# Perceiver block on one core: weight pieces split during the context, part of the output projection moved into attention

## The reference

```python
x = x + xattn(ctx, layernorm(x))   # latents attend to 8192 context tokens and to themselves
x = x + attn_layers(layernorm(x))  # 8 layers of linear attention and a 2048-wide MLP
x = x + ffn(layernorm(x))          # 16 groups of experts

def xattn(ctx, lat):               # 8 heads of 64
    q = ln(lat) @ Wq
    k, v = split(concat(ln(ctx), ln(lat)) @ Wkv)   # context keys are rotated
    return (softmax(q k^T / 8) v) @ Wo

def layer(x):
    Q, K, v = elu(x Wq + bq) + 1, elu(x Wk + bk) + 1, x Wv + bv
    V = Q * sum(K * v) / (Q * sum(K) + eps)
    x = norm(gelu(V Wo + bo) + x)
    return norm(gelu(gelu(x Wf1 + bf1) Wf2 + bf2) + x)
```

## Time and profile before

| | |
|---|---|
| median of 3 runs | 2258.04 us (2256.72 to 2260.37) |
| the profiled execution | 2262.21 us |
| its span in the profile | 2260.3 us |
| mean granted TensorE clock | 0.987 |
| TensorE matmul busy | 2143.5 us, 95% |
| VectorE busy | 1650.3 us, 73% |
| ScalarE busy | 1100.0 us, 49% |
| GpSimd busy | 992.3 us, 44% |

### The profile page before, as it was taken

How to read it: one execution, slowest core, us unless ns; L and a number is a source line. 1 busy time by engine, 2 the same in 40 slices (tenths; PEclk the granted TensorE clock), 3 DMA queues, 4 the chain that set the end, 5 groups by cost and what they waited for, 6 DMA issues and landing times. The chain is left out here.

```text
span 2260.3 us, 37940 instructions
## 1 busy us (share of the span) xinstructions
PE 2143.5 (95%) x12744; PEld 1083.5 (48%) x12843; DVE 1650.3 (73%) x2384; ACT 1100.0 (49%) x1722; POOL 992.3 (44%) x682
## 2 busy tenths in 40 slices
PE   5899999989999999999799999999999999999977
PEld 2344444433333333323365575757566575756633
DVE  7687777659989999999575756667575666757663
ACT  4122322234445544555364755646475565646545
POOL 0234434459999999978320402222040222204044
PEclk9999999999999999999899999999999999999989
DMA  3344454333333432432223333342323334233313
GB/s 115 131 150 140 152 178 143 130 120 87 114 116 91 121 102 84 121 96 81 102 87 113 94 131 104 101 142 86 113 84 131 104 118 134 76 112 97 122 38 113
DMA packets 159853, 252.74 MB, mean 112 GB/s; under 512 B 11506, under 2 KB 63986, under 8 KB 159730
## 3 DMA queue, kind: packets, MB, share of 16 engines
q1 hardware_dynamic: 159730, 250.96, 34.8%
HBM read 211.73 MB, written 36.70 MB: 110 GB/s over the span
## 5 line engine op out<-in xcount | busy, mean ns | idle before, releaser
L1345 POOL TENSOR_TENSOR l_rstd<-l_var_eps,neg_half 128x1 f32<-128x1 f32 x71 | 67.3, 948 | 835.0 <-DVE l_var_eps L1399 835.0
L66 PE MATMUL l_mm<-xt_hi,wt_hi 128*128 128x256 f16 (+3 forms) x1568 | 413.2, 275 | 6.7 <-DVE xt_lo L1388 5.6
L68 PE MATMUL l_mm<-xt_hi,wt_lo 128*128 128x256 f16 (+3 forms) x1568 | 413.1, 275 | 0.4
L67 PE MATMUL l_mm<-xt_lo,wt_hi 128*128 128x256 bf16 (+3 forms) x1560 | 410.5, 275 | 0.0
L878 DVE TENSOR_REDUCE pmax<-mx 128x1024 f32 (+1 forms) x196 | 239.3, 1221 | 29.4 <-PE mx L1069 20.0
L68 PE MATMUL l_tok<-wt_hi,h_lo 128*128 128x512 f16 x576 | 218.8, 380 | 1.7
L1627 ACT ACTIVATE wt_hi<-stage 128x512 f16<-128x512 f32 x384 | 213.6, 615 | 5.2 <-DMA stage<-in_L_attn_Wf 5.1
L1082 PE MATMUL sc<-q_hi,res 128*128 128x512 f16 x544 | 208.4, 383 | 6.4 <-ACT f_hi L992 3.2
L1083 PE MATMUL sc<-q_lo,res 65*128 65x512 f16 x544 | 207.5, 381 | 0.0
L66 PE MATMUL l_tok<-wt_hi,h_hi 128*128 128x512 f16 x512 | 194.6, 380 | 0.0
L67 PE MATMUL l_tok<-wt_lo,h_hi 128*128 128x512 bf16 x480 | 182.4, 380 | 0.0
(11 more groups left out here) (321 smaller groups left out, 4874.3 us busy)
## 6 DMA issues: line engine op xcount, KB each, us to landing
stage<-in_L_attn_Wf SPq DMA_DIRECT2D x64, 1024.0 KB, 5.2
keys<-wt_hi SPq DMA_DIRECT2D x136, 128.0 KB
res<-keys SPq DMA_DIRECT2D x68, 256.0 KB, 3.4
vb<-values SPq DMA_DIRECT2D x68, 256.0 KB, 5.6
stage<-in_ctx SPq DMA_DIRECT2D x16, 1024.0 KB, 9.8
values<-wt_lo SPq DMA_DIRECT2D x16, 1024.0 KB
stage<-in_L_ffn_f SPq DMA_DIRECT2D x16, 1024.0 KB, 5.3
res<-keys SPq DMA_DIRECT2D x68, 128.0 KB, 5.4
```

The source lines that it names most:

```text
L66: pe.matmul(out, lh, rh, start=first, stop=False, **kw)
L67: pe.matmul(out, lh, rl, start=False, stop=False, **kw)
L68: return pe.matmul(out, ll, rh, start=False, stop=last, **kw)
L1345: g.tensor_tensor(rstd[:, t:t + 1], var_eps[:, t:t + 1], k.neg_half[:, 0:1], ALU.pow).then_inc(rstd_done, 1)
```

## The change

1. **Six weight chunks are made in the context phase.** In context blocks 3, 5, 7, 9, 11 and 13 ScalarE makes the four high pieces of a chunk after its last value copy, and GpSimd the four low pieces as its last work of the block. SP loads each chunk (1 MB) into `k.res` one block earlier, after the store of the values. They are `wv`, `wo` and `wf1`, which go to slots 6 to 11. As `k.res` also holds the key buffers of attention, their constant row is written by VectorE in context block 15 instead of the first phase, and SP's first key loads wait for the last low piece. SP's loop is written out.
2. **Attention makes only three chunks, in pair 3.** Pairs 1 and 2 have no loads, high or low pieces. In pair 3 the last two low pieces stand behind the last sums.
3. **Nine twelfths of the output projection stand at attention's end.** The two score banks become shared with the layers' `mm`. TensorE projects pairs 0 and 1 of tile 0 ahead of the last row sums, and the rest of pairs 0 to 2 of all tiles behind them. The layers do pair 3 alone.
4. **Order at the layers' start.** The bias transposes go to the banks `tok`, TensorE's wait for the bias instructions goes away, and VectorE splits tiles 0 to 2 ahead of the sum of tile 3.

```diff
@@ context_phase, SP @@
+                    if u == 0 and 1 <= i <= EARLY_CHUNKS:
+                        if i > 1:
+                            sp.wait_ge(w_lo, 4 * (i - 1))
+                        sp.dma_start(k.res[:], k.first_weights(STAGES - 1 + i).rearrange("(c p) n -> p c n", p=P)).then_inc(w_in, 16)
-                over_blocks(sp, body)
+                for b in range(CTX_BLOCKS):
+                    body(b // 2, b % 2)
@@ context_phase, GpSimd, end of body @@
+                    if has_pieces(i, u):
+                        for n in range(4):
+                            pool.wait_ge(w_hi, 4 * i + n - 3)
+                            g.tensor_tensor(lo_pieces[:, piece_at(i, n), :], k.res[:, n:n + 1, :],
+                                            hi_pieces[:, piece_at(i, n), :], ALU.subtract).then_inc(w_lo, 1)
@@ context_phase, VectorE @@
+                    if isinstance(i, int) and (i, u) == (HALF_BLOCKS - 1, 1):
+                        dve.wait_ge(w_lo, 4 * EARLY_CHUNKS)
+                        for n in range(2):
+                            v.memset(k.kh[n][HD:HD + 1], M_UNIT).then_inc(units, 1)
@@ context_phase, ScalarE, end of body @@
                     values(i, u, 3)
+                    if has_pieces(i, u):
+                        act.wait_ge(w_in, 16 * i)
+                        for n in range(4):
+                            a.activation(hi_pieces[:, piece_at(i, n), :], k.res[:, n:n + 1, :], ACT.Copy).then_inc(w_hi, 1)
@@ attention_phase, VectorE @@
-                            block_work(p, b, b > FIRST_PIECE)
+                            block_work(p, b, FIRST_PIECE < b < KB - 1)
...
-                        weight_low(p, KB)
+                        for b in range(KB - 1, KB + 1):
+                            weight_low(p, b)
                         continue
-                    with dve.Fori(0, FIRST_PIECE + 1 if p else TURN) as b:
+                    with dve.Fori(0, TURN) as b:
                         block_work(p, b, False)
-                    if p:
-                        dve.wait_ge(w_staged, 16 * STAGES * p)
-                        with dve.Fori(FIRST_PIECE + 1, TURN) as b:
-                            block_work(p, b, True)
                     pair_max(p + 1)
                     for b in range(TURN, KB):
-                        block_work(p, b, p > 0)
-                    if p:
-                        weight_low(p, KB)
+                        block_work(p, b, False)
@@ attention_phase, TensorE @@
+                def project(t, c):
+                    toks = slice(t * P, (t + 1) * P)
+                    product3(t_, sc[t // 2][:, t % 2 * TOK:(t % 2 + 1) * TOK], (k.o_hi[:, c, toks], k.o_lo[:, c, toks]),
+                             (k.wt_hi[:, XWO, c, :], k.wt_lo[:, XWO, c, :]), c == 0, False)
...
+                for c in range(2):
+                    project(0, c)
                 row_sums(PAIRS - 1)
+                for t in range(TT):
+                    for c in range(0 if t else 2, PAIRS - 1):
+                        project(t, c)
@@ layers_phase, VectorE @@
                 stream_norm(1)
+                low(0, 0)
+                stream_norm(2)
+                low(1, 1)
+                low(2, 2)
                 stream_stats(3)
-                stream_norm(2)
...
                 stream_norm(3)
-                for t in range(TT - 1):
-                    low(t, t)
                 dve.sem_inc(w_lo_dve, 32)
@@ layers_phase, TensorE @@
-                    for c in range(PAIRS):
-                        x = product3(t_, mm[t][:], (k.o_hi[:, c, rows], k.o_lo[:, c, rows]),
-                                     (wt_hi[:, XWO, c, :], wt_lo[:, XWO, c, :]), c == 0, c == PAIRS - 1)
-                    x.then_inc(projected, 1)
+                    c = PAIRS - 1
+                    product3(t_, mm[t][:], (k.o_hi[:, c, rows], k.o_lo[:, c, rows]),
+                             (wt_hi[:, XWO, c, :], wt_lo[:, XWO, c, :]), False, True).then_inc(projected, 1)
...
-                pe.wait_ge(cols_done, 4)
```

More of the change, by code:

```diff
@@ L35 @@
 MAX_COLS = KB + 2
+EARLY_CHUNKS = 6
 PIECES = 4 * STAGES
@@ L181, in norm @@
                                         ALU.subtract, ALU.mult).then_inc(norm_done, 1)
-                for n in range(2):
-                    v.memset(k.kh[n][HD:HD + 1], M_UNIT).then_inc(consts, 1)
                 norm(0, k.x_sb, z, EPS_OUTER)
@@ L265, in _ @@
                 t_ = nc.tensor
-                pe.wait_ge(consts, 6)
+                pe.wait_ge(consts, 4)
                 pe.wait_ge(norm_done, 2 * TT)
@@ L357, in context_phase @@
         passed = sem("c_passed")
+        units, w_in, w_hi, w_lo = (nc.alloc_semaphore(n) for n in ("c_units", "c_w_in", "c_w_hi", "c_w_lo"))
+        k.spare_semaphores += [units, w_in, w_hi, w_lo]
+        hi_pieces, lo_pieces = (w[:].rearrange("p a c n -> p (a c) n") for w in (k.wt_hi, k.wt_lo))
         ctx_v = k.ctx.rearrange("(b t p) d -> b p t d", p=P, t=SUB)
@@ L384, in earlier_units, with has_pieces, piece_at @@
             return TT * b + (2 * TT if not isinstance(b, int) or b >= 3 else TT if b == 2 else 0)
+        def has_pieces(i, u):
+            return u == 1 and (not isinstance(i, int) or 1 <= i <= EARLY_CHUNKS)
+        def piece_at(i, n):
+            return bass.ds(4 * (XWO + STAGES - 1 + i) + n, 1)
         def late_pair(i, u):
@@ L442, in body @@
                     if not before_end(i, u, 1):
+                        sp.wait_ge(w_lo, 4 * EARLY_CHUNKS)
                         for n in range(2):
@@ L749, in attention_phase @@
         o_inv, o_t = rows(k.h_lo, 12, 2), rows(k.h_lo, 14, 2)
-        sc = [pb(f"sc{n}", [P, 2 * TOK], F32) for n in range(2)]
+        sc = k.scores
         mx = pb("mx", [P, 2, BLK], F32)
@@ L794, in load_weights @@
                 def load_weights(p, n):
-                    if not 1 <= p < PAIRS:
-                        return
-                    if p > 1:
-                        sp.wait_ge(w_lo, PIECES * (p - 2) + CH * (n + 1))
-                    c = STAGES * (p - 1) + n
-                    w = ((k.xwo, k.wk[0], k.wq_l[0], k.wv[0], k.wo[0])[c] if c < 5
-                         else k.wf1[0, :, (c - 5) * D:(c - 4) * D])
-                    sp.dma_start(k.stage[:, n], w.rearrange("(c p) n -> p c n", p=P)).then_inc(w_staged, 16)
+                    if p == PAIRS - 1:
+                        sp.dma_start(k.stage[:, n], k.first_weights(n).rearrange("(c p) n -> p c n", p=P)).then_inc(w_staged, 16)
                 def two_on(p, b):
@@ L1031, in _ @@
                         continue
-                    with act.Fori(2, FIRST_PIECE if p else TURN) as b:
+                    with act.Fori(2, TURN) as b:
                         for j in range(SUB):
                             exponential(p, b, j)
-                    if p:
-                        act.wait_ge(w_staged, 16 * STAGES * p)
-                        with act.Fori(FIRST_PIECE, TURN) as b:
-                            for j in range(SUB):
-                                exponential(p, b, j)
-                            weight_high(p, b)
                     for b in range(TURN, KB):
@@ L1228, in layers_phase @@
         kv_neg = sb("kv_neg", [P, CH], F32)
-        mm = [pb(f"l_mm{n}", [P, D], F32) for n in range(4)]
+        mm = [k.scores[n // 2][:, n % 2 * D:(n % 2 + 1) * D] for n in range(4)]
         tok = [pb(f"l_tok{n}", [P, D], F32) for n in range(2)]
@@ L2283, in perceiver_kernel @@
     k.load_k = load_k
+    k.first_weights = lambda c: ((k.xwo, k.wk[0], k.wq_l[0], k.wv[0], k.wo[0])[c] if c < 5
+                                 else k.wf1[0, :, (c - 5) * D:(c - 4) * D])
     with ExitStack() as ctx:
@@ L2302, in perceiver_kernel @@
         k.c_in = ctx.enter_context(nc.semaphore("e_c_in"))
-        with nc.sbuf_tensor("h_lo", [P, FT, TOK], BF16) as k.h_lo, ExitStack() as xattn:
+        with nc.sbuf_tensor("h_lo", [P, FT, TOK], BF16) as k.h_lo, ExitStack() as banks, ExitStack() as xattn:
             def xsb(name, shape, dt):
@@ L2321, in perceiver_kernel @@
             context_phase(k)
+            k.scores = [banks.enter_context(nc.psum_tensor(f"scores{n}", [P, 2 * TOK], F32)) for n in range(2)]
             attention_phase(k)
```

28 lines of the change are left out of this document (15 added, 13 removed).

## The result

| | before | after |
|---|---|---|
| median beside each other | 2259.20 us (4 runs, 2256.72 to 2262.71) | 2244.22 us (4 runs, 2242.10 to 2244.50) |
| ratio | | 0.9929, 95% interval 0.9914 to 0.9944 |
| the profiled execution | 2262.21 us | 2242.10 us |
| its span | 2260.3 us | 2240.3 us |
| mean granted TensorE clock | 0.987 | 0.987 |

The change takes off 2259.20 - 2244.22 = 15.0 us by the medians. Dividing the two medians gives 0.9934, inside the interval of the ratio. The forecast was 16.8 off, 2241.2; the measured 2244.22 lies inside its range, and the change is faster, as forecast. The two profiled executions are 20.0 us apart, more than the medians, so a milestone table is wanted before any term is judged. Each number is the start, from the start of the span, of one instruction in the timelines.

A forecast was written before the change was run, and what follows sets the result against it. TensorE was taken to bound the context and attention without pieces, VectorE attention with pieces. Attention's 9.4 us and the entry's 7.4 make 16.8 off the median 2258.04: 2241.2 us, range 2237.5 to 2246.5.

The forecast's parts named there:

- Pieces out of pairs 1 and 2: Attention, blocks 3 to 15: without pieces each pair falls from 107.88 to 104.64 us, 3.24 gained in each.
- Handovers: Attention: pair 1 to pair 2 gains 1.69 us, pair 2 to pair 3 gains 1.2 (bounds 0.3 and 2.3).
- The context at nothing: Context blocks: the added pieces fit GpSimd's wait to a tenth of a us and cost 0 (bounds -0.5 and +3).
- Rival 2: Context: the subtractions' fit fails or the extra load delays a block, 0.5 us six times, 2244.2 us; chance 0.10.
- The end of attention: Last row sums start 0.6 us earlier, but 30 projection matmuls follow, so the layers begin about as before: worth nothing.
- The entry: Passage into the layers: first sum 4.45 us earlier, first matmul of layer 0 7.6, loads 7.2; taken as 7.4.
- the last part of the entry: Last normalisation to layer 0's first matmul: 5.34 us becomes 0.4, while splits and their waits add 1.95 and 1.3 earlier.
- rival 1: Layers' start: three splits ahead of tile 3's sum stop VectorE's chain, entry gives 5 us, 2243.6 us; chance 0.14.
- Rival 3: Layers' start: the projection did not hold the entry, so only attention's 9.4 us stay, 2248.6 us; chance 0.05.
- Rival 4: Context: GpSimd's subtractions hold VectorE's products 3.4 us through the shared port, six times, slower at 2261.6 us; chance 0.03.

The follow-up runs named there:

- e5: e0 with each of GpSimd's 24 low-piece subtractions in the context made twice, same output; 2246.94 us, ratio 0.9938 to the kernel before.
- e7: e0 with all 48 projection matmuls back in the layers, early splits and free bias banks kept; 2251.13 us, ratio 0.9960 to the kernel before.
- e0: The changed kernel with GpSimd's loop over the context blocks written out, control for other experiments; 2248.42 us, ratio 0.9939 to the kernel before.
- e2: The kernel before with only the projection, bias banks and order of splits changed, pieces left in pairs 1 to 3; 2252.72 us, ratio 0.9963.
- e3: e0 with the three splits put back behind the last normalisation; 2247.26 us, ratio 0.9937 to the kernel before.
- e1: e0 with projection, bias banks and splits as before, so only the pieces move to the context; 2250.44 us, ratio 0.9951 to the kernel before.
- e6: e0 with ScalarE's four high pieces ahead of its last two value copies; 2243.99 us, ratio 0.9930 to the kernel before.
- e8: e0 with ScalarE's rounding of an earlier pair's output two steps later in pair 3's blocks; 2244.99 us, ratio 0.9926 to the kernel before.
- e9: e0 with layer 0's release signal right after the third split and e8's later rounding; 2240.80 us, ratio 0.9908 to the kernel before.

## Why the prediction was right

**Pieces out of pairs 1 and 2 (3.24 + 3.24): exact.** Both came out as 107.88 - 104.64. The count and the pattern block were both in the trace of before, in the same pair.

**Handovers (1.69 and 1.2): 2.16 and 1.31.** The first took 46.97 us in the kernel after and the 47.44 of the pattern, to 0.02, in the nine experiments with short pairs, so 1.69 is what the change gives and the other 0.47 belongs to that one execution; where it comes from is open. The second is read between block 15 and block 16 of pair 2 (9.49 to 8.18); the lead stays the same from there to block 4 of pair 3. Its size is right and its make-up is partly luck: the prediction took 0.77 for this block, down to 8.72, and the rest for the last piece behind it. The block went to 8.18, and behind it nothing came. Attention's sum until then is 9.95 us where 9.4 stood.

**The context at nothing: right, for a safer reason than the one given.** Blocks stayed at 24.18. The prediction had the subtractions fit to a tenth of a us, from a duration of the layers. They took 1.12 us each, and 0.61 was left; and e5 shows that even 3.8 us too much would have cost 0.1 to 0.2 us a chunk. Rival 2's price of 0.5 was several times too high. Its reason against, that TensorE needs the keys only a block later, is what e5 measured.

**The end of attention (0.6 worth nothing): right.** The row sums stand 9.47 us after the last block's start instead of 9.85, and the layers still begin no earlier: their lead falls from 13.54 to 12.91, because the projection now ends behind the last split.

**The entry (7.4): 20.50 - 12.91 = 7.59 for layer 0's first matmul.** The first sum is 17.38 - 12.91 = 4.47 earlier (4.45 predicted), and e7 gives the projection 4.65. Both reasons given, fewer matmuls and a TensorE that comes to them from work, show in e7: there the twelve matmuls of tile 0 come at half the pace of the same instructions in the kernel after. The chain from there to the last normalisation took 13.01 (12.8 predicted), and 0.26 was left behind it (0.4). Layer 0 does start at the lower level, as foreseen: its 384-column matmuls start every 0.32 us from 1089.93 on, behind a window at 0.56.

**What was wrong in it.** First, pair 3 was put at nothing behind its start, and the change costs about 1.1 us there. From block 4 to block 8 pass 35.40 us before and 36.53 in `e0`, with a mean granted clock of 0.90 and 0.91 in the stretch; in e2, which has the old pairs 1 and 2, 33.73, and in the kernel after 34.88, both at 0.95. The code of these blocks is the same. The stop of 0.97 us in block 4 stands in all eight traces that have short pairs 1 and 2 and the old place of the rounding, and in neither of the two with the long pairs. Why the short pair 2 leads to it is open. Second, the last part of the entry was credited to the wrong work. The step set 5.34 us of transposes, roundings and splits against 1.95 and 1.3 of new work in the chain and gave the difference, 5.34 - 0.4 - 1.95 - 1.3 = 1.7, to the splits' early place. e3 gives them 0.29, and leaves 5.34 - 3.86 = 1.48 for TensorE's removed wait for the bias instructions, which the prediction did not price at all (1.7 by e7 and e1; no run isolates it). The sum held because the two belong to the same stretch.

**The rivals.** The splits did wait (0.78 and 0.36 us, 1.14 for two, beside the 1.3 taken), not 3 us in all: rival 1 falls. Rival 3 falls with e7. Rival 4, the port, has a true mechanism for another instruction than the one it named: e6 shows VectorE held 2.55 us when GpSimd's subtractions stand beside its normalisation. It doesn't decide, because in the kernel after the normalisation ends 0.70 us before they start, and because even in e6 the price is 0.2 us a chunk, not 3.4: the products wait for TensorE anyway. The Trainium skill (SBUF — State Buffer, Who interferes with whom) says that a VectorE instruction with at most one SBUF input, outside the two-port modes, leaves GpSimd alone; the trace agrees, with products at 1.41 us beside the subtractions as without them. The prediction gave this exemption without its condition on the two-port modes, and the condition matters: the normalisation has one SBUF input too, and e6 shows it held.

**16.8 against 15.0 by the medians.** The ratio's interval, 0.9914 to 0.9944, is 12.7 to 19.4 us of 2259.20, so it holds both numbers. By the traces the stretch from block 15 of pair 0 to layer 0 is 9.95 + 0.91 (pair 3 until the row sums) - 0.63 + 7.59 = 17.8 us shorter in the kernel after, and 496.05 - 480.34 = 15.7 in `e0`. The two differ by the 0.47 of the handover and by blocks 4 to 7 of pair 3, 34.88 and 36.53 us, where the clock stood higher in the kernel after. `e0` has the mean clock of the kernel before in these blocks, so 15.7 compares like with like: 16.8 for the terms that were forecast, less the 1.1 of pair 3 that wasn't. That these terms come to 16.8 to a tenth is partly luck: the second handover and the last part of the entry came out at their sizes by other work than was named. The medians add what executions of the same code differ by, 2.4 us among those of the kernel after and 6.0 among those before. Three places of it are known: the first phase (95.37 to 98.07), the four blocks of pair 3 (33.3 to 36.5 with short pairs), and everything from layer 0's first matmul to the end (1150.0 to 1152.9 us over the twelve traces). Which of these the medians hold can't be told from one profile of each.

## What to carry to other kernels

Move work off the stage whose bound engine it delays into one where the bound engine waits for none of it, and ask less whether it fits a gap than when its consumer needs the result: here a missed gap cost a twentieth of its length. When an accumulation waits for its last operand, let an idle TensorE add the other terms ahead of it; that saves their time, and here it kept the clock up (1.00 against 0.57 when the last matmuls came). Before crediting a reordering, undo it alone: a wait that was removed beside it may have done the work.

## What was not expected

**The same stop of TensorE was followed by a lower clock in most executions, and in one by none.** All traces but those of e8 and e9 have a stop of 2.35 to 2.37 us in pair 3. Behind it, windows of `e0` and of e6:

```profile
990.00:995.00 5.00, 5.00 (x13) 1.47 (x13) 4.90 (x4) 2.72 (x4) 4.76 (x4) 0.50 0.00 0
```

```profile
990.00:995.00 5.00, 3.89 (x17) 1.23 (x18) 4.80 (x5) 4.31 (x6) 3.63 (x3) 1.00 0.01 3
```

The granted clock is 0.50 in the one and 1.00 in the other; in the kernel after it was 0.75. From block 4 to block 8 pass 36.53, 33.29 and 34.88 us, with the same code. So the stops cost about 33.29 - 31.61 = 1.7 us against e8 where the clock stays up, and 36.53 - 33.29 = 3.2 more where it falls. The Trainium skill (TensorE: Matmul & The Clock Gate, Part 1: The HAM clock gate) has the ratio set by how busy the array has been recently; the windows of `e0` and of the kernel after agree, and e6 shows that one such stop does not always lower it.

**GpSimd's subtraction has two durations.** It took 1.12 us in the context and 1.304 in the layers, for the same shape. What stands beside it differs (products of VectorE here, splits of weights with two SBUF operands there), but no run separates that from the rest.

**The start of attention depends on the clock too.** Between 479 and 484 us the granted clock was 1.00 before and 0.51 after, with TensorE busy 3.42 and 4.90 us:

```profile
479.00:484.00 5.00, 4.90 (x12) 1.69 (x13) 0.00 (x0) 2.05 (x3) 1.82 (x1) 0.51 0.36 135
```

The lead was 2.61 us in the context and 2.68 at block 3 of pair 0, so it cost nothing between these two traces. In e8 it did: 3.2 us, as told there.
